# Cross attention's scores by a seven-product block form over pairs of key chunks

## The reference, cut to what matters

```python
Q = jnp.einsum('bqe,fe->bqf', x, Wq) + bq                 # 512 x 1024
K = k_cache[:, :end_step, :]                              # 8192 x 1024, the last 512 rows are projected from x
V = v_cache[:, :end_step, :]
scores = jnp.einsum('bqe,bke->bqk', Q, K) * scale + attention_mask
attn = jax.nn.softmax(scores, axis=-1)
return jnp.einsum('bqk,bke->bqe', attn, V)
```

## Time and profile before

| | |
|---|---|
| median of 3 runs | 1389.62 us (1389.3 to 1390.12) |
| the profiled execution's own time | 1388.84 us |
| its span in the profile | 1387.2 us |
| TensorE (PE) busy | 1366.7 us, 99% |
| VectorE (DVE) busy | 892.5 us, 64% |
| ScalarE (ACT) busy | 531.3 us, 38% |
| GpSimd (POOL) busy | 196.8 us, 14% |
| mean granted clock | 1.0 |

### The profile page before, as it was taken

How to read it: one execution, slowest core, us unless ns; L and a number is a source line. 1 busy time by engine, 2 the same in 40 slices (tenths; PEclk the granted TensorE clock), 3 DMA queues, 4 the chain that set the end, 5 groups by cost and what they waited for, 6 DMA issues and landing times. The chain is left out here.

```text
span 1387.2 us, 18236 instructions
## 1 busy us (share of the span) xinstructions
PE 1366.7 (99%) x6424; PEld 1121.5 (81%) x6424; DVE 892.5 (64%) x1297; ACT 531.3 (38%) x947; POOL 196.8 (14%) x276
## 2 busy tenths in 40 slices
PE   7999999999999999999999999999999999999999
PEld 6878888888888888888888888877777888888887
DVE  6666466566665566665666657686766676677665
ACT  3333232323323233223232222555532435666561
POOL 3001000000000000000000000344422022122123
PEclk9999999999999999999999999999999999999999
DMA  7467365554555544555544452900510466898766
GB/s 251 155 210 249 103 205 168 172 179 159 167 169 168 180 164 164 169 168 175 172 159 167 143 184 73 281 4 30 214 36 30 154 198 220 307 318 295 255 241 215
DMA packets 101645, 245.06 MB, mean 177 GB/s; under 512 B 10400, under 2 KB 56032, under 8 KB 89120
## 3 DMA queue, kind: packets, MB, share of 16 engines
q1 hardware_dynamic: 87408, 185.11, 39.6%
q0 software_dynamic: 11296, 48.94, 10.7%
q10 hardware_dynamic: 2880, 10.22, 1.9%
HBM read 203.07 MB, written 41.16 MB: 176 GB/s over the span
## 5 line engine op out<-in xcount | busy, mean ns | idle before, releaser
L37 PE MATMUL banks<-V_hi,b_PT_hi 128*128 128x512 f32 x512 | 199.3, 389 | 0.0
L39 PE MATMUL banks<-V_hi,b_PT_lo 128*128 128x512 f32 x512 | 199.2, 389 | 0.0
L38 PE MATMUL banks<-V_lo,b_PT_hi 128*128 128x512 f32 x512 | 199.2, 389 | 0.0
L37 PE MATMUL banks<-K_hi,QT_hi 128*128 128x512 f32 x512 | 199.2, 389 | 0.0
L38 PE MATMUL banks<-K_lo,QT_hi 128*128 128x512 f32 x512 | 199.2, 389 | 0.0
L39 PE MATMUL banks<-K_hi,QT_lo 128*128 128x512 f32 x512 | 199.2, 389 | 0.0
L1163 ACT ACTIVATE b_PT_hi<-b_p_in 128x512 fp32r<-128x512 f32 x63 | 39.8, 632 | 297.9 <-DMA b_p_in<-pt_dram 297.9
L1397 DVE TENSOR_TENSOR b_scores<-banks,b_scores 128x512 f32<-128x512 f32 x64 | 44.3, 691 | 169.5 <-PE banks L39 169.5
L726 POOL DMA_DIRECT2D b_scores<-mask x62 | 33.3, 537 | 651.3 <-DVE b_turned L1346 632.3
L2343 DVE TENSOR_TENSOR e_lo<-e_raw,e_hi 128x1024 fp32r<-128x1024 f32 x80 | 95.1, 1231 | 35.5 <-ACT e_hi L2170 34.7
L37 PEld LDWEIGHTS banks<-K_hi,QT_hi 128*128 128x128 f32 x512 | 96.2, 188 | 20.1
(11 more groups left out here) (339 smaller groups left out, 2763.6 us busy)
## 6 DMA issues: line engine op xcount, KB each, us to landing
raw<-kv SPq DMA_DIRECT2D x60, 1024.0 KB, 4.9
e_raw<-w_up SPq DMA_DIRECT2D x40, 512.0 KB, 5.0
e_raw<-w_down SPq DMA_DIRECT2D x40, 512.0 KB, 6.2
b_scores<-mask POOLq DMA_DIRECT2D x64, 256.0 KB, 3.0
pt_dram<-b_turned SPq DMA_DIRECT2D x63, 256.0 KB, 2.0
b_p_in<-pt_dram SPq DMA_DIRECT2D x252, 64.0 KB, 2.0
d_s_raw<-shared_w SPq DMA_DIRECT2D x26, 512.0 KB, 4.4
raw<-xattn_w SPq DMA_DIRECT2D x11, 1024.0 KB, 6.5
```

The lines of the kernel that those rows point to most:

```text
L37: pe.matmul(out, lhs_hi, rhs_hi, start=first, stop=False)
L38: pe.matmul(out, lhs_hi, rhs_lo, start=False, stop=False)
L39: return pe.matmul(out, lhs_lo, rhs_hi, start=False, stop=last)
```

## The change

The chunks are taken in pairs. A pair's scores are a product of two by two blocks: 256 queries or the other 256, the first 512 features or the last, 512 keys or the other 512. That product of 8 block products is made with 7, in the form with 15 block additions. Each of the seven (`product`) is 2 query tiles by 4 feature blocks by 3 passes, 24 matmuls, taken in two halves of the features. What it needs:

- Sums and differences of query blocks (`q1` to `q4`), once, on GpSimd at the end of `cross_projections`: eight additions of 128x1024; they are split once (`queries_hi`, `queries_lo`).
- Differences of key blocks for each pair: four, in two halves each. GpSimd makes `combine(0)` and `combine(1)`, VectorE `combine(2)` and `combine(4)`, each instruction 128x1024.
- Fourteen halves of key blocks to split for each pair instead of four quarters of 128x2048 (`keys_hi`, `keys_lo`, 128x1024 each), into a ring of three slots `k_hi`, `k_lo`. One key block is loaded twice (`x2_again`).
- The first product's result is copied out of PSUM by ScalarE (`copy_first`); GpSimd adds it to six mask tiles (`offer`), VectorE adds two of the products to two of these (`hold`); the other additions are made in PSUM, by matmuls that go on adding to a bank (`onto`).

The values product keeps its 24 matmuls a step. The turned probabilities, `b_p_in` and the raw values now have one buffer each. The order of each engine is written out for a pair of chunks (`pair_of_chunks`) and run eight times. VectorE's is shown with several calls to a line and as it stands from the second pair on; in the first pair `queries_lo(0)` and `queries_lo(1)` follow `combine(2, s_)`, and `queries_lo(2)` and `queries_lo(3)` the second `turn`.

More of the change, by code:

```diff
@@ L472, in route_rows, with attention @@
     return mm
[L475 to L476 removed]
+def attention(nc, block, m, ins, resid, QT, K, V, X, raw, PT, at, in_loaded, raw_loaded, ident, y_cleared, ln, d, F, weff,
+              weff_stored, own, pt_dram, y_dram):
     QT_hi, QT_lo = QT
@@ L548, in raw_tile, with O_ps, role @@
-        def raw_tile(u):
-            n = W if u % TB < 2 else D
-            return raw[:, u % 2, :].rearrange("p (b n) -> p b n", n=n)
+        def O_ps(n):
+            return bank[:, 4 + 2 * (n % 2):6 + 2 * (n % 2), :].rearrange("p h n -> p (h n)")
+        def role(r, s):
+            return 3 if r == "y2" else (s + {"x1": 0, "x2": 1, "y1": 2}[r]) % 3
+        loads, count = {}, list(raws_before)
+        for s_ in range(PAIRS_OF_CHUNKS):
+            for r in ("x1", "x2", "y1", "y2", "x2_again"):
+                if s_ == 0 and r in ("x1", "x2", "x2_again"):
+                    continue
+                i = role("y1" if r == "x2_again" else r, s_)
+                count[i] += 16
+                loads[r, s_] = count[i]
@@ L642, in clear_rows @@
                           zeros[:, :].unsqueeze(1).to_broadcast([P, (MAXC - MINC) * DB, P])).then_inc(y_cleared, 16)
-        def passes(engine, step, after):
-            for u in range(BODY):
-                step(0, u, u)
-            with engine.Fori(1, STEPS // BODY - 1) as it:
-                for u in range(BODY):
-                    step(it * BODY, u, BODY)
-            last = STEPS - BODY
-            for u in range(BODY):
-                step(last, u, last + u)
-            after(STEPS)
@@ L899, in step, with left @@
-            def step(base, u, known):
-                scores(base, u, known)
-                if known >= 2:
-                    values(base, u - 2, known - 2)
+            def left(i, t, f):
+                tile = slice(t * P, (t + 1) * P)
+                if i in (2, 3, 6):
+                    return [x[:, f, tile] for x in (X["q2_split"], X["q3_split"], X["q4_split"])[(2, 3, 6).index(i)]]
+                e, tile = {0: (f, 2 + t), 1: (4 + f, 2 + t), 4: (4 + f, t), 5: (f, t)}[i]
+                return [x[:, e, tile * P:(tile + 1) * P] for x in (QT_hi, QT_lo)]
@@ new lines, in _ @@
+            for s_ in range(PAIRS_OF_CHUNKS):
+                pair_of_chunks(s_)
+            weights_lo(0)
+            values_lo(4 * PAIRS_OF_CHUNKS - 1)
+            accumulate(STEPS - 5)
+            pt_lo(STEPS - 4)
+            weights_lo(1)
+            pt_lo(STEPS - 3)
+            accumulate(STEPS - 4)
+            pt_lo(STEPS - 2)
+            add_x(0)
+            accumulate(STEPS - 3)
+            pt_lo(STEPS - 1)
+            normalize(0)
+            add_x(1)
+            accumulate(STEPS - 2)
```

825 lines of the change are left out of this document (557 added, 268 removed).

## The result

The changed kernel takes 1496.97 us, the median of 4 runs (1494.85 to 1498.76), against 1389.87 of the kernel before beside it: a ratio of 1.077, with an interval of 1.0751 to 1.0789. The forecast was 1398 us and its range ended at 1418. The direction was right, the size was not: the change costs 107 us and not 8.

What follows compares the result with a forecast made beforehand. TensorE, busy 99%, bounds the kernel, so removing matmuls helps only while other engines stay ahead. Start 16 + passages 31 + end 5 - saving 43.5 = +8.5 us, forecast 1398 us, range 1372 to 1418 for 8 in 10.

Steps and rivals of the forecast that it cites:

- The saving: Cross attention, 8 pairs: 192 matmuls go, a pair takes 81.6 us instead of 87.0, 43.5 us saved if TensorE never waits.
- The start: First pair: third product 13 us late, fourth waits 3, sum 16; the fifth's 4.5 is counted in the later stretch.
- The end: Last pair: values step n + 4 follows at once while VectorE still has work, 5 us.
- Seven passages at 4.5 us, 31 us in all: From fourth product to next pair's `pt_lo(n - 3)`: VectorE's stretch 64.3 us against TensorE's 59.8, seven times, less 0.8.
- They take turns: VectorE's two-SBUF-operand operations and GpSimd's alternate; a GpSimd operation of d costs a waiting VectorE d - 0.2.
- the forecast's 8.0: VectorE's loss beside GpSimd per passage, over two row sums, value half, `pt_lo(n - 4)`, two key halves; 7.4 after 0.6 hides.
- the price of a load of probabilities, 3.3 us everywhere: In the deciding stretch: load of probabilities taken as 3.3 us, giving 1.5 us of waits for late high parts.
- a queue falls behind as well: Rival, chance 0.08: all of GpSimd's work meets VectorE, 10.7, or SP's loads fall behind too; 1423 us.
- the tightest low part at n+2: Within the deciding stretch, `pt_lo(n + 2)` is the tightest low part and comes 0.4 us late.
- Granted clock stays 1.00: Whole kernel: TensorE's clock is not lowered by the new waits, as in the rest with 10 us of idle TensorE.
- With contention taken away: Rival, change pays, chance 0.30: no loss to GpSimd gives 17 - 43.5 = -26.5, 1363 us.
- Which operations wait: VectorE beside GpSimd: operations with two SBUF operands (`combine`, key splits) wait, those with a PSUM operand run normally.

Runs made afterwards that it cites:

- third run: GpSimd's arithmetic made small and 15/16 of the key and value load bytes left out, against the changed kernel: 1378.91 us.
- number 12: V_lo of step n-4 put ahead of the accumulation of n-6 on VectorE, against the kernel with only the loads exchanged (1460.84): 1432.01 us.
- numbers 4 and 5: Changed kernel with GpSimd's second difference waiting for the low part of n-4; the former also issues two probabilities' loads earlier: 1431.19 and 1465.98 us.

## Why the prediction was wrong

*The saving.* Right. 192 matmuls fewer, and where nothing else interferes a pair takes 82.3 us (third run), against 81.6 and the 82.0 of the forecast's list. VectorE has the time for the work as a mean.

*The start.* Right: 13.5, 2.2 and 4.3 us of stall, forecast 13, 3 and 4.5. GpSimd's 128x1024 operation was priced at 2.35 us and takes 2.37 to 2.40, and there the two did take turns. What it left out was the slower matmuls between the stalls: the fifth product is 23.2 us late, where 13 + 3 + 4.5 = 20.5 was forecast. The end: a stall of 5.2 us, forecast 5; but with the waits of 1.1 at the turnings, the slower matmuls and whatever the account leaves over it comes to 11.7.

*Seven passages at 4.5 us, 31 us in all.* This is the step that failed. They cost 7 x (97.9 - 81.6) = 114 us, and three terms of it were wrong.

The first is a statement, "They take turns". The earlier trace rows have single GpSimd operations beside VectorE; the forecast carried this over to four operations in a row and let VectorE in between. In the changed kernel it was not let in: the value half lost 6.6 us instead of 1.55. With the two row sums (1.8 and 0.4) VectorE lost 8.8 us, near the forecast's 8.0; but nearly all of it fell into one operation, straight ahead of the low part that TensorE waits for, and the stall became 7.3 to 9.0 us instead of 4. The other operations to which the forecast gave a part of the loss, `pt_lo(n - 4)` and two key halves, lost nothing: the row was over when they came. The runs with GpSimd late or small put it at 31 to 83 us of the kernel; the lower one collides elsewhere, and the upper one has some 6 us of the start in it (its fifth product starts at 191.75).

The second is the price of a load of probabilities, 3.3 us everywhere. Five of the eight in a pair stand close behind a 1 MB load and take 4.5 to 7.9 us to land; the two of them that cost TensorE a stall, n+3 and n-1, took up to 7.9. The forecast had named this ("a queue falls behind as well") but only as a part of a rival at 0.08, and gave it no time of its own. It looked for the tightest low part at n+2; in the changed kernel TensorE waits at n+3. Small loads give back 38.9 us, the exchange of two issues 36.1.

The third is "Granted clock stays 1.00". It rested on the rest of the kernel, whose idle time comes in pieces of at most 1.09 us. The long stalls here are followed by a stretch at 0.50, which adds 2.0 to 4.5 us to a pair with some 9 to 13 us of stalls. That the clock is the cause of the extra time is read from the durations (0.63 instead of 0.39); no run held it fixed.

*The rivals.* With contention taken away the forecast had 1363; the third run gives 1378.91, since its fifth product (190.60) is 16.2 us late and not 9, and the end and the rest behind it take some 7 us more. Which operations wait is as forecast: in number 12 the two accumulations from PSUM beside GpSimd's subtraction keep their 1.27 us each (2.46 together), and the two-SBUF operations wait. The Trainium skill (SBUF — State Buffer, Who interferes with whom) says that a VectorE instruction with two SBUF inputs contends with a GpSimd instruction that reads SBUF, and one with at most one SBUF input does not; the trace agrees. That a waiting operation may have to wait for a whole row, rows 7, with single operations of GpSimd, could not show.

*Left open.* Why some rows of GpSimd operations let nothing in while others alternate. That the row began undisturbed is not enough, as the start of the changed kernel shows; the size of VectorE's operation, between 2048 and 1024 elements, is ruled out; a real gap in the row was not achieved. What all the closed rows share is a DMA issue of GpSimd directly ahead of them. That is read from the traces only: no run moved the DMA issue alone, and the wait added in numbers 4 and 5 stands between it and the row, so there two things changed at once.

## What to carry to other kernels

An engine with spare time is no free helper if its operations hold up those of the engine that others wait for. Let them run beside operations that they don't delay (here those with a PSUM operand), and place a row of them behind the critical operation, not in front. Order the small load that someone waits for ahead of the big one that nobody waits for yet; the exchange of two lines gave 36 us here. And when a change makes the bounding engine wait, price the stall with the slower matmuls behind it.

## What the runs showed of the hardware

- A VectorE operation with two SBUF operands that asked while GpSimd was in a row of four such operations, begun right behind a DMA issue, waited for the rest of the row (8.87 us instead of 2.29, of 7.2 us of row); of two halves the first took up to 7.83 us. The same in the projections of the changed kernel: beside a row of four GpSimd additions from 126.86 to 136.32, an operation of 2.29 us that asked in the third took 5.57.
- Where GpSimd's first operation had had to wait for VectorE, the two alternated, operation by operation (4.53 and 6.62 us for two each; low part 2.77). They did so too in rows that began undisturbed but not right behind a DMA issue (158.38 in the changed kernel: GpSimd's third took 3.32 us instead of 2.4). Which of the differences between the rows decides is not shown.
- Even a 128x1 operation with SBUF operands waits for a GpSimd operation: 1.95 us instead of the 0.18 that it takes elsewhere in the changed kernel.
- A 256 KB load in four parts, issued 1.8 us behind a 1 MB load on the same queue, took 7.4 us to its user instead of 3.3.
- After TensorE had waited 7.58 us the granted clock was 0.50, and 1.00 again some 3.4 us after it went on; after 0.89 us only the first matmul took longer (0.50 us instead of 0.39).
